# Output weights of an attention block asked for earlier, between the transposes of the last head

## The chip, the cores and the metric

The kernel runs on one core of one Trainium2 chip. The metric is the device time of one execution in microseconds (us). The core has a matrix engine (TensorE, PE), a vector engine (VectorE, DVE), an activation engine (ScalarE, ACT), a general engine (GpSimd, POOL) and a sync engine (SyncE, SP) whose queue issues DMA transfers. Each engine runs its own instructions in order; semaphores tie them together.

## The reference

A transformer block on x of 1 x 2048 x 512 in float32: modulation vectors from a conditioning vector, layer norm, causal attention with 16 heads of 128, its output projection and residual, a second layer norm, and a mixture of 64 experts (top 4) with shared experts. The change touches only the end of the attention:

```
q, k, v = h @ Q_w[hd] + Q_b[hd], h @ K_w[hd] + K_b[hd], h @ V_w[hd] + V_b[hd]     # per head hd, 16 heads
p    = softmax(where(causal, q @ k.T / sqrt(128), -1e5))
attn = p @ v                                                                       # 2048 x 128 per head
x    = x + ga * (sum over hd of attn[hd] @ O_w[hd] + O_b)                          # O_w[hd]: 128 x 512
```

## The kernel before, in words

Every product is made from high and low parts with three matmuls (`matmul3`, L1696 to L1698). A head is worked in four stages j = 0 to 3, one for each block of 512 query rows. In a stage, TensorE first computes the scores of block j (`strip`), then the attended values of block j-1 (`sum_values`, written to `pv`), then q, k and v of the next block (`gen`). VectorE takes the scores out of PSUM with their maxima (L1257, L1263, L1267), ScalarE takes exponentials in place (`exps`, L935) and writes the high half of the probabilities (`p_hi`, L944), VectorE the low half (`p_lo`, L1281). Both halves are transposed by DMA into `pT` (L500, `turn_first_rows` for the first two of the four row tiles, `turn_last_rows` for the others), and v by another (L528, `turn_values`). ScalarE takes attended values out of `pv` into the single buffer `at_f` (L950, `attended`), which it may overwrite only once the store of the block before has landed (`at_stored`; L533, `store_at`). In ScalarE's order q and k of the next block (L922, L924) come behind that, and VectorE's `kT_lo` (L1210) behind those; the scores of the next stage need it.

All of these transfers stand in the queue of SyncE, in the order in which the code writes them, and so do the 16 output weight tiles `O_w[hd]`, 256 KB each (`load_wo`, L560). They go through three raw buffers (`wq_raw`, `wk_raw`, `wv_raw`, tile hd in buffer hd % 3), so the request for tile hd first waits until GpSimd has split tile hd-3 (`wo_split`). GpSimd's split is a cast (L834) and a subtraction (L836) into `wo`; tiles 0 to 7 may be written once v of block 0 of the last head is computed, tiles 8 to 15 once v of its block 3 is. While a request waits, nothing behind it in SyncE's queue is issued.

The last head is head 15, written (15, j) below for its stage j. After the scores of (15, 3) and the attended values of (15, 2), TensorE begins the output projection: 16 row tiles i, each the sum over 16 heads, 48 matmuls of `wo` and `a_hi`/`a_lo`. Row tile i = 0 waits for `wo_split` of hd + 1 before each head's three matmuls, the last of them for tile 15. Then come i = 1, the attended values of (15, 3), i = 2 and so on. The attended heads are read back from `at_dram` in units u of four heads (`load_a`, L584 into `a_early` for u < 6, L588 into the two buffers `a_f` after that), and split by ScalarE (`take_a`, L1021, which waits for `a_used` of four units before) and VectorE (`split_a`, L1432). ScalarE takes out the attended values of (15, 3) behind unit 11, SyncE stores them and then loads x again for the residual (`load_xo`, L591), on which GpSimd adds a bias row by row (L843), on which VectorE's sum (L1446) waits.

Of the kernel before, what the change touches and what calls it, by code (L numbers as in the profile page):

```python
# [41 lines left out]
def adaln_block(nc, x, Q_w, Q_b, K_w, K_b, V_w, V_b, O_w, O_b, Wr, router_bias, Wg, Wu, Wd, Sg, Su, Sd,  # L42
                c_in, wmod, out):
    _, S, D = x.shape
    H, _, DH = Q_w.shape
    E, _, HE = Wg.shape
    NS, _, HS = Sg.shape
    TOPK = 4
# [18 lines left out]
    with ExitStack() as ctx:  # L67
# [122 lines left out]
        def wo_raw(hd):  # L190
            return raw[hd % WOS][:].rearrange("p c d -> p (c d)")
# [186 lines left out]
        def groups_before(j):  # L378
            return j * (j + 1) // 2
# [9 lines left out]
        def slot_free(n, h):  # L389

            before = n + GROUPS - PTS if n >= PTS else n + (GROUPS - 1 - n) // PTS * PTS
            return h * GROUPS + (before + 1)
# [66 lines left out]
        def _(sp):  # L459
            def wait_alone(semaphore, value):  # L460

                sp.wait_ge(semaphore, value)
                sp.sem_inc(sp_waited, 1)
# [32 lines left out]
            def turn_pair(h, j, r, g, part):  # L496

                rows = (p_hi16, p_lo16)[part][:, g, 2 * r:2 * r + 2, :].rearrange("p t c -> p (t c)")
                out = pT[:, slot_of(j, g), part, 2 * r:2 * r + 2].rearrange("p t k q -> p (t k) q")
                sp.dma_start_transpose(out, rows).then_inc(p_turned[slot_of(j, g)], 16)  # L500

            def turn_first_rows(h, j):

                wait_alone(p_hi, h * NT + (TB * j + 2))
                for g in range(j + 1):
                    wait_alone(pv_group, slot_free(groups_before(j) + g, h))
                    turn_pair(h, j, 0, g, 0)
                if j == 1:
                    turn_values(h, 1, h)
                wait_alone(p_lo, h * NT + (TB * j + 2))  # L510
                for g in range(min(j + 1, QB - 1)):
                    turn_pair(h, j, 0, g, 1)

            def turn_last_rows(h, j):
                wait_alone(p_hi, h * NT + (TB * j + 4))
                for g in range(j + 1):
                    if g == QB - 1:
                        turn_pair(h, j, 0, g, 1)
                    turn_pair(h, j, 1, g, 0)
                    if g == 0:  # L520
                        wait_alone(p_lo, h * NT + (TB * j + 4))
                    turn_pair(h, j, 1, g, 1)

            def turn_values(h, j, ready):
                wait_alone(gen_out, nth("v", j, ready) + GENS)
                if j == 0 and not (isinstance(h, int) and h == 0):
                    wait_alone(pv_group, h * GROUPS + (groups_before(QB - 1) + 1))
                sp.dma_start_transpose(v16[:, j].rearrange("p n t d -> p (n t) d"), vT16[:].rearrange("p n c -> p (n c)")  # L528
                                       ).then_inc(v_turned, 16)

            def store_at(h, j):
                wait_alone(at_ready, h * QB + (j + 2))
                sp.dma_start(at_dram[bass.ds(h, 1), :, 512 * j:512 * j + 512].rearrange("o p s -> (o p) s"), at_f[:]  # L533
                             ).then_inc(at_stored, 16)
# [20 lines left out]
            def load_wo(hd):  # L555
                if hd < WOS:
                    sp.wait_ge(w_split, 3 * H)
                else:
                    sp.wait_ge(wo_split, hd - WOS + 1)
                sp.dma_start(wo_raw(hd), O_w[hd]).then_inc(wo_landed[hd % WOS], 16)  # L560

            turn_first_rows(H - 1, 1)
            turn_last_rows(H - 1, 1)
            for hd in range(6):
                load_wo(hd)
            store_at(H - 1, 0)
            turn_values(H - 1, 2, H - 1)
            for hd in range(6, 9):
                load_wo(hd)
            turn_first_rows(H - 1, 2)  # L570
            for hd in range(9, 12):
                load_wo(hd)
            turn_last_rows(H - 1, 2)
            store_at(H - 1, 1)
            turn_values(H - 1, 3, H - 1)
            load_wo(12)

            at_parts = at_dram.rearrange("(n h) p s -> n p h s", h=HH)

            def load_a(u):  # L580
                i, part = u // TU, u % TU
                src = at_parts[part][:, :, P * i:P * i + P]
                if u < EARLY:
                    sp.dma_start(a_early[:, u], src).then_inc(a_early_landed[u], 16)  # L584
                    return
                if u >= EARLY + AFS:
                    sp.wait_ge(a_split, u - AFS + 1)
                sp.dma_start(a_f[:, u % AFS], src).then_inc(a_landed[u % AFS], 16)  # L588
# [27 lines left out]
            sp.wait_ge(at_stored, 16 * (QB * h + 2))  # L616
            for u in range(EARLY):
                load_a(u)
            for hd in range(13, H):
                load_wo(hd)  # L620
            turn_first_rows(h, j)
            sp.wait_ge(strip_done, NSTRIP * H)
            for u in range(EARLY, EARLY + AFS):
                load_a(u)
            turn_last_rows(h, j)
            store_at(h, QB - 2)
            sp.wait_ge(wo_split, H - 1)
            sp.dma_start(gob[:], O_b.partition_broadcast(P)).then_inc(ob_landed, 16)
            for u in range(EARLY + AFS, UNITS):
# [1436 lines left out]
```

## Time and profile before

| what | value |
|---|---|
| median of 3 runs | 2032.54 us (2032.47 to 2037.23) |
| profiled execution, its own time | 2040.55 us |
| its span | 2038.9 us |
| PE busy | 1942.8 us (95%) |
| DVE, ACT, POOL busy | 1422.5, 1121.6, 568.8 us |
| mean granted TensorE clock | 0.985 |

TensorE is busy for 95% of the span. In the profile's 40 slices of 51 us its busy digit is 9 nearly everywhere; the lowest after the beginning is a 6 in the slice from 1274 to 1325 us, where the clock's digit is 7 too, and the slice behind it has an 8. These two hold the last stages of head 15 and the start of the output projection. Before 1226 us the heads repeat one pattern; the stages of head 15 begin with its scores at 1227 us (stage 0), 1246 (stage 1), 1260 (stage 2) and 1287 (stage 3). The output projection begins at 1317 us.

In a timeline row the columns are start, duration, engine, line and tiles, and in brackets the idle time before it and what ended that. A row with SPq is the issue of a DMA on SyncE's queue.

### The profile page before, as it was taken

To read this page: it belongs to the slowest core of one execution; us is meant where nothing else is said; L and a number is where in the kernel's file an instruction comes from. 1 tells how busy PE (TensorE), PEld (TensorE's weight loads), DVE (VectorE), ACT (ScalarE), POOL (GpSimd) and SP (SyncE) were. 2 spreads that over 40 slices of the span, in tenths; PEclk is the share of its full clock that TensorE was granted. 3 is DMA by queue.
4 is the path that set the end of the run, shared out by engine and by line. 5 is a ranking of instruction groups with operands and counts; after the bars stand their busy time and mean duration, and the time that the engine had idled before them with its cause. 6 is when DMAs were issued, how large, how long until landed. Compare 5 with 4: busy or idle time off the path is not lost.

```text
span 2038.9 us, 33861 instructions
## 1 busy us (share of the span) xinstructions
PE 1942.8 (95%) x9821; PEld 1147.9 (56%) x9821; DVE 1422.5 (70%) x3593; ACT 1121.6 (55%) x1638; POOL 568.8 (28%) x585
## 2 busy tenths in 40 slices
PE   5899999999999999999999999689999999999998
PEld 2444444444444444444444444368877778777786
DVE  5787797797797797797797797546545843333477
ACT  3576776776676676676676676413333144344311
POOL 5430330330330330330330311632000132222265
PEclk8999999999999999999999999799999999999999
DMA  6278777777777777777777777874431098999676
GB/s 237 64 173 176 172 173 176 172 173 176 172 172 176 173 172 176 178 168 176 175 171 176 172 156 160 206 207 142 124 109 32 1 294 276 314 293 312 223 209 185
DMA packets 932246, 366.68 MB, mean 180 GB/s; under 512 B 754800, under 2 KB 885920, under 8 KB 932128
## 3 DMA queue, kind: packets, MB, share of 16 engines
q1 hardware_dynamic: 921888, 331.93, 64.9%
q0 software_dynamic: 10240, 33.56, 5.3%
q14 instruction: 90, 0.74, 0.1%
q8 instruction: 28, 0.46, 0.1%
HBM read 138.86 MB, written 41.94 MB: 89 GB/s over the span
## 4 chain that ended last, share of the span: by engine, by line
PE 66%; DVE 8%; DMA 6%; SPq 6%; issue 6%; POOL 4%; ACT 3%; DVEq 0%; ACTq 0%; POOLq 0%
PE gen L1696 9%; PE gen L1697 9%; PE gen L1698 9%; PE strip L1696 6%; PE strip L1698 6%; PE strip L1697 6%; PE pv L1697 5%; PE pv L1696 5%; PE pv L1698 5%; SPq L500 5%; PE strip L2005 4%; DMA wd_sb<-in_L_ffn_Wd 3%; DVE p_lo L1281 2%; PE strip L2012 2%; POOL gath L887 2%
## 5 line engine op out<-in xcount | busy, mean ns | idle before, releaser
L935 ACT ACTIVATE exps<-exps,nbias,cols_now 128x128 f32<-128x128 f32 (+15 forms) x256 | 329.8, 1288 | 176.2 <-DVE cmin L1267 174.2
L1281 DVE SCALAR_TENSOR_TENSOR p_lo<-exps,rinv,p_hi 128x512 f16<-128x512 f32 (+3 forms) x256 | 404.5, 1606 | 26.2 <-ACT p_hi L944 25.2
L944 ACT ACTIVATE p_hi<-exps,rinv 128x512 f16<-128x512 f32 (+3 forms) x256 | 335.4, 1352 | 37.2 <-issue 15.7
L1257 DVE TENSOR_SCALAR_CACHE_REDUCE exps<-strip 128x512 f32<-128x512 f32 x384 | 250.9, 687 | 128.2 <-PE strip L1698 127.2
L1696 PE MATMUL strip<-kT_hi,qT_hi 128*128 128x512 f16 (+3 forms) x640 | 221.1, 350 | 30.7 <-DVE kT_lo L1210 21.6
L1696 PE MATMUL pv<-pT,v 128*128 128x512 f16 (+3 forms) x640 | 223.3, 349 | 3.5 <-DMA pT<-p_lo 3.5
L1697 PE MATMUL strip<-kT_lo,qT_hi 128*128 128x512 f16 (+3 forms) x640 | 223.6, 349 | 0.0
L1697 PE MATMUL pv<-pT,v 128*128 128x512 f16 (+3 forms) x640 | 223.3, 349 | 0.0
L1698 PE MATMUL strip<-kT_hi,qT_lo 128*128 128x512 f16 (+3 forms) x640 | 221.2, 349 | 0.0
L757 POOL TENSOR_TENSOR wq_f<-wq_f,fac 128x512 f32<-128x512 f32 x16 | 16.7, 1041 | 730.7 <-PE gen L1698 726.8
L1698 PE MATMUL pv<-pT,v 128*128 128x512 f16 (+3 forms) x640 | 219.8, 349 | 0.0
L1120 ACT ACTIVATE xbT<-gen,modT,scale_b 128x128 f32<-128x128 f32 x256 | 96.4, 457 | 89.2 <-PE gen L1997 89.2
L1696 PEld LDWEIGHTS strip<-kT_hi,qT_hi 128*128 128x128 f16 x640 | 62.7, 98 | 118.0 <-issue 36.5
L1263 DVE CUSTOM_DVE_ANT_0 exps<-strip,causal 128x128 f32<-128x128 f32 (+3 forms) x256 | 124.6, 487 | 5.2 <-PE strip L1698 2.4
L1642 DVE TENSOR_TENSOR hE<-strip,sil_e 128x128 f32<-128x128 f32 x64 | 18.7, 292 | 150.2 <-ACT sil_e L1127 84.9
L1696 PE MATMUL gen<-wo,a_hi 128*128 128x512 f32 x256 | 101.5, 396 | 10.7 <-DVE a_lo L1432 5.7
L950 ACT ACTIVATE at_f<-pv,at_bias,at_scale 128x512 f32<-128x512 f32 x64 | 49.0, 765 | 105.6 <-PE pv L1698 98.2
L1021 ACT ACTIVATE a_hi<-a_f 128x512 fp32r<-128x512 f32 x58 | 36.6, 632 | 123.3 <-DMA a_f<-at_dram 86.6
L1696 PEld LDWEIGHTS pv<-pT,v 128*128 128x128 f16 x640 | 62.8, 98 | 70.1 <-issue 5.6
L1696 PE MATMUL gen<-hT_hi,wq_hi 128*128 128x512 f16 x256 | 97.7, 382 | 3.7 <-issue 3.7
L1697 PE MATMUL gen<-wo,a_hi 128*128 128x512 f32 x256 | 100.5, 393 | 0.0
L1698 PE MATMUL gen<-wo,a_lo 128*128 128x512 f32 x256 | 100.4, 392 | 0.0
(266 smaller groups left out, 4309.5 us busy)
## 6 DMA issues: line engine op xcount, KB each, us to landing
at_dram<-at_f SPq DMA_DIRECT2D x64, 256.0 KB, 2.5
wg_sb<-in_L_ffn_Wg SPq DMA_DIRECT2D x64, 256.0 KB
wu_sb<-in_L_ffn_Wu SPq DMA_DIRECT2D x64, 256.0 KB
wd_sb<-in_L_ffn_Wd SPq DMA_DIRECT2D x64, 256.0 KB
yb_dram<-yb SPq DMA_DIRECT2D x64, 256.0 KB
a_f<-at_dram SPq DMA_DIRECT2D x58, 256.0 KB, 2.8
pT<-p_hi SPq DMA_TRANSPOSE x320, 2.7
pT<-p_lo SPq DMA_TRANSPOSE x320, 2.8
```

Of the source, the lines that this page charges most:

```text
L500: sp.dma_start_transpose(out, rows).then_inc(p_turned[slot_of(j, g)], 16)
L935: nc.scalar.activation(row, row, ACT.Exp, bias=nbias[:, t:t + 1], scale=cols_now[:, LOGIT_UP:LOGIT_UP + 1], accum_out=rsum[:, t:t + 1]).th ...
L944: nc.scalar.activation(p_hi16[:, 0:j + 1, t, :], row, ACT.Copy, scale=rinv[:, t:t + 1]).then_inc(p_hi, 1)
L950: nc.scalar.activation(at_f[:], pv[:], ACT.Identity, bias=at_bias[:, 0:1], scale=at_scale[:, 0:1]).then_inc(at_ready, 1)
L1120: ins = nc.scalar.activation(xbT[:, i % 2, P * ch:P * ch + P], e_turn[:, P * ch:P * ch + P], ACT.Identity, bias=modT[:, 3 * DC + ch:3 * DC ...
L1257: nc.vector.tensor_scalar(exps[:, t, 512 * ch:512 * ch + w], strip[u % STRIPS][:, 0:w], 1.0, None, ALU.mult, ALU.max, accum_out=cmax[:, t, ...
L1263: nc.vector.tensor_tensor_reduce(exps[:, t, 512 * ch:512 * ch + w], strip[u % STRIPS][:, 0:w], causal[:, TB * P - w:TB * P], 1.0, -3e38, A ...
L1281: nc.vector.scalar_tensor_tensor(p_lo16[:, 0:j + 1, t, :], row, rinv[:, t:t + 1], p_hi16[:, 0:j + 1, t, :], ALU.mult, ALU.subtract).then_i ...
L1696: nc.tensor.matmul(o, a_hi, b_hi, start=start, stop=False)
L1697: nc.tensor.matmul(o, a_hi, b_lo, start=False, stop=False)
L1698: return nc.tensor.matmul(o, a_lo, b_hi, start=False, stop=stop)
L2005: last = nc.tensor.matmul(e_gateup[i % 2][:, P * n:P * n + P], w[:, i % EX, c, :], xbT[:, i % 2, P * c:P * c + P], start=c == 0, stop=c == ...
```

## The change

The order of SyncE's queue changes in the last head; no instruction is added or taken away. Requests for weight tiles now stand as follows: tiles 0 to 2 ahead of the first transposes of (15, 1); 3 and 4 between its first and last ones; 5 to 7 behind the store of (15, 0) and the transposition of v; 8 and 9 between the first and last transposes of (15, 2); 10 to 12 behind the six `a_early` loads; 13 and 14 behind the two `a_f` loads, between the first and last transposes of (15, 3); and 15 behind its last ones and the store of (15, 2).

```diff
+            for hd in range(3):
+                load_wo(hd)
             turn_first_rows(H - 1, 1)
+            for hd in range(3, 5):
+                load_wo(hd)
             turn_last_rows(H - 1, 1)
-            for hd in range(6):
-                load_wo(hd)
             store_at(H - 1, 0)
             turn_values(H - 1, 2, H - 1)
-            for hd in range(6, 9):
+            for hd in range(5, 8):
                 load_wo(hd)
             turn_first_rows(H - 1, 2)
-            for hd in range(9, 12):
+            for hd in range(8, 10):
                 load_wo(hd)
             turn_last_rows(H - 1, 2)
             store_at(H - 1, 1)
             turn_values(H - 1, 3, H - 1)
-            load_wo(12)
...
             for u in range(EARLY):
                 load_a(u)
-            for hd in range(13, H):
+            for hd in range(10, 13):
                 load_wo(hd)
             turn_first_rows(h, j)
             sp.wait_ge(strip_done, NSTRIP * H)
             for u in range(EARLY, EARLY + AFS):
                 load_a(u)
+            for hd in range(13, 15):
+                load_wo(hd)
             turn_last_rows(h, j)
             store_at(h, QB - 2)
+            load_wo(H - 1)
             sp.wait_ge(wo_split, H - 1)
```

SyncE's queue before, from the end of the transposes of (15, 1) to the transposition of v for (15, 2):

```order
L500 DMA_TRANSPOSE pT<-p_lo_118 128x8x128
L560 DMA wq_raw<-in_L_attn_O_w 128x512
L560 DMA wk_raw<-in_L_attn_O_w 128x512
L560 DMA wv_raw<-in_L_attn_O_w 128x512
L560 DMA wq_raw<-in_L_attn_O_w 128x512
L560 DMA wk_raw<-in_L_attn_O_w 128x512
L560 DMA wv_raw<-in_L_attn_O_w 128x512
L533 DMA at_dram<-at_f 128x512
L528 DMA_TRANSPOSE v_113<-vT_114 128x8x128
```

Six requests stood ahead of the store of (15, 0), the last three of them with a wait for GpSimd. The same place now, from the end of the first transposes of (15, 1):

```order
L500 DMA_TRANSPOSE pT<-p_lo_118 128x8x128 x2
L560 DMA wq_raw<-in_L_attn_O_w 128x512
L560 DMA wk_raw<-in_L_attn_O_w 128x512
L500 DMA_TRANSPOSE pT<-p_hi_117 128x8x128
L500 DMA_TRANSPOSE pT<-p_lo_118 128x8x128
L500 DMA_TRANSPOSE pT<-p_hi_117 128x8x128
L500 DMA_TRANSPOSE pT<-p_lo_118 128x8x128
L533 DMA at_dram<-at_f 128x512
L528 DMA_TRANSPOSE v_113<-vT_114 128x8x128
L560 DMA wv_raw<-in_L_attn_O_w 128x512
L560 DMA wq_raw<-in_L_attn_O_w 128x512
L560 DMA wk_raw<-in_L_attn_O_w 128x512
```

The two requests shown first are tiles 3 and 4; the store now follows the transposes directly. The queue before, around the first transposes of (15, 3), where tiles 13 to 15 were requested:

```order
L584 DMA a_early<-at_dram 128x4x128 x6
L560 DMA wk_raw<-in_L_attn_O_w 128x512
L560 DMA wv_raw<-in_L_attn_O_w 128x512
L560 DMA wq_raw<-in_L_attn_O_w 128x512
L500 DMA_TRANSPOSE pT<-p_hi_117 128x8x128 x4
L500 DMA_TRANSPOSE pT<-p_lo_118 128x8x128 x3
L588 DMA a_f<-at_dram 128x4x128 x2
L500 DMA_TRANSPOSE pT<-p_hi_117 128x8x128
```

The last of the three `wq_raw`/`wk_raw`/`wv_raw` rows is tile 15. The end of the last transposes of (15, 3) now:

```order
L500 DMA_TRANSPOSE pT<-p_lo_118 128x8x128 x2
L500 DMA_TRANSPOSE pT<-p_hi_117 128x8x128
L500 DMA_TRANSPOSE pT<-p_lo_118 128x8x128
L533 DMA at_dram<-at_f 128x512
L560 DMA wq_raw<-in_L_attn_O_w 128x512
L632 DMA gob<-in_L_attn_O_b 128x512
L589 DMA a_f<-at_dram 128x4x128 x5
```

The `wq_raw` row is tile 15; it has moved behind all 16 transposes of (15, 3), two `a_f` loads and the store of (15, 2).

## Rows read from the trace of the kernel before

**Rows 1.** Windows by stage: stretch, length, busy (instructions) of PE, PEld, DVE, ACT, POOL, clock, DMA, GB/s.
```profile
1287.09:1299.04 11.95, 11.85 (x48) 5.01 (x48) 9.12 (x38) 3.84 (x4) 5.43 (x7) 0.82 0.97 225
1302.56:1312.26 9.70, 9.70 (x36) 4.04 (x36) 2.23 (x1) 4.26 (x3) 2.39 (x2) 0.70 1.04 224
1317.45:1330.62 13.17, 13.17 (x49) 10.71 (x49) 11.77 (x8) 6.92 (x8) 10.41 (x6) 0.82 1.02 209
1330.62:1341.50 10.88, 10.88 (x49) 8.82 (x48) 0.69 (x1) 0.63 (x1) 0.00 (x0) 1.00 1.02 188
1341.50:1350.88 9.38, 9.38 (x49) 4.55 (x49) 1.39 (x2) 1.26 (x2) 1.27 (x1) 1.00 0.60 144
```

**Rows 2.** Timeline of PE: start, duration, engine, line, tiles, idle time before.
```profile
1287.09 0.61 PE L1696 MATMUL strip<-kT_hi,qT_hi 128*128 128x512 f16 x1 [8.00 <-DVE kT_lo L1210]
...
1302.56 0.58 PE L1696 MATMUL pv<-pT,v 128*128 128x512 f16 x1 [3.53 <-DMA pT<-p_lo]
...
1317.45 0.77 PE L1696 MATMUL gen<-wo,a_hi 128*128 128x512 f32 x1 [5.02 <-issue]
...
1341.50 0.39 PE L1696 MATMUL pv<-pT,v 128*128 128x512 f16 x1
...
1367.32 0.50 PE L1696 MATMUL gen<-wo,a_hi 128*128 128x512 f32 x1 [2.54 <-DVE a_lo L1432]
```

**Rows 3.** Timeline of ACT in the last head.
```profile
1267.62 3.04 ACT L944 ACTIVATE p_hi<-exps,rinv 128x1536 f16<-128x1536 f32 x2 [1.42 <-issue]
...
1284.23 0.78 ACT L950 ACTIVATE at_f<-pv,at_bias,at_scale 128x512 f32<-128x512 f32 x1 [7.44 <-issue]
...
1308.00 3.89 ACT L944 ACTIVATE p_hi<-exps,rinv 128x2048 f16<-128x2048 f32 x2 [11.23 <-DMA pT<-p_lo]
...
1315.85 1.13 ACT L1021 ACTIVATE a_hi<-a_early 128x512 fp32r<-128x512 f32 x2
```

**Rows 4.** Timeline of SyncE's DMA issues in the last head.
```profile
1265.65 0.58 SPq L560 DMA_DIRECT2D wq_raw<-in_L_attn_O_w x1
...
1280.41 0.33 SPq L560 DMA_DIRECT2D wv_raw<-in_L_attn_O_w x1
1280.85 0.36 SPq L533 DMA_DIRECT2D at_dram<-at_f x1
...
1286.62 4.01 SPq L500 DMA_TRANSPOSE pT<-p_hi x3
...
1314.30 0.43 SPq L560 DMA_DIRECT2D wq_raw<-in_L_attn_O_w x1
...
1340.82 0.50 SPq L533 DMA_DIRECT2D at_dram<-at_f x1
```

**Rows 5.** Waits of SyncE, 1200 to 1400 us: total, times, longest.
```profile
SPq L560 <- POOL wo L836: 15.3, 6, 5.0
```

**Rows 6.** Tile `wo`: GpSimd's casts and subtractions, ns least/median/most, first and last start.
```profile
L834 POOL CAST wo<-wv_raw x5: 607/611/2677, 1275.4 to 1319.7; 128x512 fp32r<-128x512 f32 x5
L836 POOL TENSOR_TENSOR wo<-wv_raw,wo x5: 1264/1266/2653, 1277.7 to 1322.5; 128x512 fp32r<-128x512 f32 x5
```

**Rows 7.** Line L560 (weight requests), 1264 to 1270 us, then 1312 to 1330: time to landing.
```profile
DMA to landing us min/median/max: 3.0/3.3/3.7
...
DMA to landing us min/median/max: 4.5/4.5/4.7
```

**Rows 8.** Timeline of POOL: the split of tile 0 and the end of tile 15's.
```profile
1269.46 2.72 POOL L836 TENSOR_TENSOR wo<-wq_raw,wo 128x512 fp32r<-128x512 f32 x1
...
1326.81 1.62 POOL L836 TENSOR_TENSOR wo<-wq_raw,wo 128x512 fp32r<-128x512 f32 x1
```

**Rows 9.** Timeline of DVE: low halves in stages (15, 1) and (15, 2).
```profile
1256.11 2.58 DVE L1281 SCALAR_TENSOR_TENSOR p_lo<-exps,rinv,p_hi 128x1024 f16<-128x1024 f32 x2
...
1269.23 1.82 DVE L1281 SCALAR_TENSOR_TENSOR p_lo<-exps,rinv,p_hi 128x1536 f16<-128x1536 f32 x1
```

**Rows 10.** Chain that ended last, 1341 to 1363 us: start, duration, what.
```profile
1352.85 0.77 ACT at_f L950
...
1354.10 8.27 DMA acc<-in_L_attn_x
```

## The prediction

> **What bounds the kernel now.** I read the table of 40 slices first, since PE is busy for 95% of the span and only a hole in its row can be won: the hole is at 1274 to 1350 us, the last stages of head 15. Then the timeline of PE there, for what ended each idle time [rows 2]: 8.00 us ahead of the scores of (15, 3), 3.53 ahead of the attended values of (15, 2), 5.02 ahead of the output projection, 16.6 us together. The windows by stage [rows 1] show that each gap is followed by a stretch at a mean granted clock of 0.82, 0.70 and 0.82, between the levels 2.4 and 1.2 GHz; that loses 0.18 x 11.95 + 0.30 x 9.70 + 0.18 x 13.17 = 7.4 us. So 24 us is the most that this stretch could give.
>
> The waits of SyncE [rows 5] and its issues [rows 4] name the cause of the first gap: weight requests wait 15.3 us for GpSimd's splits, the sixth request (tile 5) is out at 1280.41, and the store of (15, 0) behind it at 1280.85. `at_f` may be overwritten only after that store, so ScalarE stands 7.44 us up to 1284.23 [rows 3], and q and k of block 3 stand behind it. From 1286.62 on SyncE has no wait of weight on requests left: it is the transposes that fill its queue up to the store of (15, 2), 1286.62 to 1340.82 + 0.50 = 1341.32 [rows 4], 54.7 us. ScalarE's 11.23 us up to 1308.00 are a wait for them [rows 3].
>
> **Moving tiles 0 to 7.** The store of (15, 0) no longer stands behind waiting requests. The three requests ahead of the first transposes of (15, 1) cost nothing, since SyncE was waiting there for `p_hi`. Tiles 3 and 4 need the splits of 0 and 1, which land some 3 us after 1248 and take 0.61 + 1.27 us each [rows 6, 7]: done by about 1257, before SyncE comes to them at 1259. They cost 2 x 0.5 us of issue ahead of the last transposes. ScalarE's first `p_hi` of (15, 2) idled 1.42 us [rows 3] and I read this as a wait for those transposes, so it starts 1 us later and its second row tile is ready at 1267.62 + 3.04 + 1.0 = 1271.7. The first transposes of (15, 2) go at 1271.8 instead of 1286.62. The store now goes at about 1267; ScalarE is then free for `at_f` when its own `p_hi` are done, 7 us earlier less the 1 us. What is late next is SyncE itself.
>
> **The queue from there on.** Between the first transposes of (15, 2) and the store of (15, 2) the queue holds the same before and after: 29 transposes, 8 loads of attended values, 2 stores, 7 weight requests (before 9 to 15, now 8 to 14). With the durations of before the store ends at 1271.8 + 54.7 = 1326.5. Without any congestion it is 29 x 1.34 (4.01 for three, rows 4) + 17 x 0.58 (the longest plain issue in rows 4) = 48.7 us, so 1320.5. I take 1324.5, between them: the loads that crowd the rings, six units of `a_early` and three weights, still stand directly ahead of transposes.
>
> **Moving tile 15.** This is the edit that decides. Before, tile 15 was requested at 1314.30 [rows 4], ahead of the transposes of (15, 3), and its split ended at 1326.81 + 1.62 = 1328.43 [rows 8], 2.2 us before row tile 0 of the projection ended at 1330.62 [rows 1]. It now stands behind all those transposes and the store. Requested at 1324.5; landing 3.0 to 4.7 us [rows 7], I take 3.6, nearer to the row measured behind transposes; split 0.61 + 0.08 + 1.27 = 1.96 [rows 6]: ready at 1330.1. TensorE needs it much sooner. The last transposes of (15, 2) are issued 8.1 + 1.0 + 8.1 = 17.2 us after 1271.8 and land some 2 us after that, 1291.1, so `p_hi` of (15, 3) comes 16.9 us earlier than 1308.00, `a_hi` at 1315.85 - 16.9 = 1299 [rows 3], the projection at 1300.6 instead of 1317.45 [rows 2]. Its row tile 0 gets to head 15 at about 1314 and stands 16 us. In place of three gaps there is one of the same size.
>
> **The sum.** From 1330.1 TensorE has 3 matmuls of head 15 and 48 of row tile 1, at 10.88 / 48 = 0.227 us [rows 1] 11.6 us, and restarts at the low level: the stretches after the three gaps lost 2.15, 2.9 and 2.4 us, I take 2.3. The attended values of (15, 3) start at 1330.1 + 13.9 = 1344.0; before 1341.50 [rows 2]. That is 2.5 us late. They take 9.38 us [rows 1].
>
> Something comes back behind them. Before, they ended at 1350.88 but ScalarE took them out at 1352.85 [rows 10], since in its order they stand behind unit 11, whose load SyncE could not ask for before 1341. These loads now start at about 1325 and are there; `at_f` comes at 1344.0 + 9.38 + 0.25 = 1353.6, 0.8 us later than before. This instruction releases the store, the load of x (8.27 us, rows 10) and GpSimd's bias, and VectorE's sums behind that are what TensorE idles for at 1367.32 (2.54 us, rows 2) and twice more shortly after. So TensorE's own 2.5 us are taken out of those idles and 0.8 us stays. Nothing later is touched. In the profiled execution's terms 2040.55 + 0.8 = 2041.4; the median of the runs is 8.0 us below that execution, and I put the same 0.8 on it: 2033.3 us.
>
> **Bounds.** Low: store at 1320.5, landing 3.0, split 1.96, 11.6, no clock loss: 1337.1, 4.4 before 1341.50, with the 1.7 of the loads (1352.85 less 1350.88 + 0.25) 6.1 early. High: 1326.5, landing 4.7, both GpSimd operations at their contended ends 0.61 + 2.65 = 3.3 [rows 6], 11.6, clock 2.9: 1349.0, 7.5 late less 1.7 is 5.8 late. So 2026.4 to 2038.3.
>
> The landing time has a second price. Beside the 3.0 to 4.7 us measured, the Trainium skill (DMA: Bandwidth & Descriptors, the anatomy of one DMA) fits about 2.0 us plus the bytes over 436 GB/s for the other path of issue, which for 256 KB is 2.6 us, by estimate. By that, tile 15 would be 1.0 us earlier and the forecast 2032.3; the rows show no landing under 3.0, so the trace does not agree.
>
> **Rivals.**
>
> *GpSimd's splits collide with VectorE in stage (15, 1): slower.* Splits of tiles 0 to 2 now fall at 1251 to 1260 us, where VectorE has no idle time and makes `p_lo` [rows 9]. A subtraction of GpSimd that met `p_lo` of 1269.23 took 2.72 us against 1.27 [rows 6, 8, 9], ending about 1.2 us after it: one holds the other off. If three subtractions each hold VectorE for their 1.27 us, the chain to `p_hi` of (15, 2) is 3.8 us later, and one starved split in front of a waiting request (2.7 us) is added to SyncE's queue. All of it goes onto tile 15: 0.8 + 3.8 + 2.7 = 7.3 us slower, 2039.8. It decides as soon as the first transposes of (15, 2) go later than about 1277. Against it: the wait for landing there hides the first 1 us or more, and TensorE's slack behind. The Trainium skill has this as a rule (SBUF — State Buffer, the shared pair of ports: a VectorE instruction with two SBUF inputs and a GpSimd one that reads SBUF exclude each other for the whole instruction); so far the trace agrees, with 2.72 against 1.27.
>
> *Tile 15 is not what TensorE waits for: faster.* Then row tiles 0 and 1 run from 1300.6 to about 1323, the attended values of (15, 3) follow as their transposes land and end near 1333, 17 us before 1350.88: 2032.5 - 17 = 2015.5. For it: all gaps of rows 2 are closed. Against it: even the uncongested queue gives the request no earlier than 1320.5, and row tile 0 can't end without that tile. To be over 6.1 us faster needs it about 1 us sooner than my lowest case, with no clock loss.
>
> *The store was not what ScalarE stood for at 1284.23* (the row names no releaser). Then the gap ahead of (15, 3) stays and the projection starts at about 1311 instead of 1300.6; but it stands for tile 15 all the same, and the end is as forecast, 2033.3 or 1 us more by what `p_hi` of (15, 3) would be late.
>
> **Chances.** Forecast 0.68, collision 0.15, faster 0.09, store not the cause 0.08. A change of 0.3%, 6.1 us, is about what can be told from none. Beyond it to the slow side lie most of the collision's case and 0.03 of the forecast's tail: 0.16. Beyond it to the fast side 0.08 and 0.02: 0.10. Within it 0.74. The range: the forecast's own bounds, drawn in a little below and reaching on the slow side to the collision, 2027 to 2039.5.
>
> **What would show it.** Right: the store of (15, 0) at about 1267; no idle time over 3 us ahead of the scores of (15, 3) and none ahead of the attended values of (15, 2); the projection starting near 1301; one idle time of TensorE of 12 to 18 us inside its row tile 0, ended by GpSimd's split of tile 15 out of `wq_raw` at 1327 to 1334, and a granted clock under 0.9 after it; SyncE with less than 3 us of waits for GpSimd in all. Wrong: that idle time under 8 us, or the split of tile 15 before 1322; or `p_lo` of (15, 1) stretched beyond 1.27 us a piece and the scores of (15, 3) not before 1286. And wrong in the last step, if the load of x comes later than `at_f` explains, or TensorE keeps its idle times at 1367 us beside the later start.

## The result, and the profile after

The changed kernel takes 2041.98 us (median of 20 executions, 2036.35 to 2045.09); the kernel before, run beside it on the same chip, takes 2038.72 us (20 executions, 2032.47 to 2041.54). The ratio is 1.0016 with a 95% interval of 1.0009 to 1.0023: some 3.3 us slower, within the 0.3% that was named as no change. Forecast were 0.8 us more, on a base of 2032.5 us. The base was wrong by itself: it was the median of three executions, and 20 have their median 6 us higher. The profiled executions are 2040.55 us before and 2043.57 us after (spans 2038.9 and 2042.0), which is 3.0 us more; the traces can be compared directly, except that the one of after runs 0.47 us late already at the store of (14, 3), 1247.83 against 1247.36.

The timeline of PE after, for the places of [rows 2]; in the brackets the idle time before the instruction and what ended it:

```profile
1262.60 0.39 PE L1700 MATMUL strip<-kT_hi,qT_hi 128*128 128x512 f16 x1 [2.43 <-DVE kT_lo L1214]
...
1284.07 0.39 PE L1700 MATMUL strip<-kT_hi,qT_hi 128*128 128x512 f16 x1 [2.49 <-DVE kT_lo L1214]
...
1303.42 0.47 PE L1700 MATMUL gen<-wo,a_hi 128*128 128x512 f32 x1 [1.01 <-issue]
...
1312.04 0.50 PE L1700 MATMUL gen<-wo,a_hi 128*128 128x512 f32 x1 [0.89 <-POOL wo L840]
...
1314.81 0.47 PE L1700 MATMUL gen<-wo,a_hi 128*128 128x512 f32 x1 [1.81 <-POOL wo L840]
...
1320.01 0.80 PE L1700 MATMUL gen<-wo,a_hi 128*128 128x512 f32 x1 [4.11 <-POOL wo L840]
...
1334.10 0.80 PE L1700 MATMUL gen<-wo,a_hi 128*128 128x512 f32 x1 [10.54 <-POOL wo L840]
...
1348.22 0.39 PE L1700 MATMUL pv<-pT,v 128*128 128x512 f16 x1
...
1375.43 0.50 PE L1700 MATMUL gen<-wo,a_hi 128*128 128x512 f32 x1 [1.22 <-DVE a_lo L1436]
```

The gaps of 8.00 and 3.53 us are gone: 2.43 us stand ahead of the scores of (15, 2), 2.49 us are left ahead of the scores of (15, 3) and none ahead of the attended values of (15, 2). The projection starts at 1303.42 instead of 1317.45, 14 us earlier, and then stands 17.6 us in its row tile 0, each time for a split of `wo`; the last and longest, 10.54 us, is for tile 15. The attended values of (15, 3) begin at 1348.22, against 1341.50 before. The windows by stage (length, busy and count of PE, PEld, DVE, ACT, POOL, then clock, DMA share, GB/s) say the same, to be read beside [rows 1]: stage (15, 3)'s scores and what follows, the projection up to tile 15, and the rest of it.

```profile
1284.07:1303.42 19.35, 18.24 (x85) 8.44 (x85) 17.00 (x53) 13.94 (x13) 3.85 (x5) 0.91 1.02 248
1303.42:1334.10 30.68, 13.07 (x46) 8.73 (x46) 12.28 (x8) 6.07 (x8) 16.60 (x13) 0.70 0.94 204
1334.10:1347.10 13.00, 13.00 (x47) 10.53 (x48) 2.76 (x4) 2.53 (x4) 1.24 (x1) 0.80 0.22 63
```

TensorE is busy for 13.07 of 30.68 us in the second, at a mean granted clock of 0.70, and works the third at 0.80.

SyncE's issues after, for [rows 4]: start, duration, line, what is issued and how often.

```profile
1268.24 0.51 SPq L533 DMA_DIRECT2D at_dram<-at_f  x1
...
1273.51 3.94 SPq L500 DMA_TRANSPOSE pT<-p_hi  x3
...
1300.29 7.21 SPq L500 DMA_TRANSPOSE pT<-p_hi  x4
...
1315.37 3.15 SPq L500 DMA_TRANSPOSE pT<-p_lo  x1
...
1328.32 0.51 SPq L533 DMA_DIRECT2D at_dram<-at_f  x1
1328.87 0.43 SPq L560 DMA_DIRECT2D wq_raw<-in_L_attn_O_w  x1
```

The store of (15, 0) goes 12.6 us earlier than in [rows 4], and the first transposes of (15, 2) 13.1 us earlier. But from them to the end of the store of (15, 2) it is 1328.83 - 1273.51 = 55.3 us, no less than the 54.7 before. The request of tile 15, at 1314.30 before, is out at 1328.87. Of what waited 15.3 us in [rows 5] nothing is left: the waits of SyncE after show no wait of a weight request for GpSimd. What GpSimd does (timeline of POOL, for [rows 8]) is this:

```profile
1254.26 2.13 POOL L840 TENSOR_TENSOR wo<-wk_raw,wo 128x512 fp32r<-128x512 f32 x1
...
1258.02 2.13 POOL L840 TENSOR_TENSOR wo<-wv_raw,wo 128x512 fp32r<-128x512 f32 x1
...
1332.09 0.61 POOL L838 CAST wo<-wq_raw 128x512 fp32r<-128x512 f32 x1 [10.24 <-DMA wq_raw<-in_L_attn_O_w]
1332.78 1.26 POOL L840 TENSOR_TENSOR wo<-wq_raw,wo 128x512 fp32r<-128x512 f32 x1
...
1365.95 24.94 POOL L847 TENSOR_TENSOR acc<-acc,gob 128x512 f32<-128x512 f32 x16 [30.61 <-DMA acc<-in_L_attn_x]
```

and ScalarE (timeline of ACT, for [rows 3] and [rows 10]):

```profile
1270.30 3.04 ACT L948 ACTIVATE p_hi<-exps,rinv 128x1536 f16<-128x1536 f32 x2 [1.62 <-issue]
...
1279.38 0.76 ACT L954 ACTIVATE at_f<-pv,at_bias,at_scale 128x512 f32<-128x512 f32 x1
...
1293.23 3.88 ACT L948 ACTIVATE p_hi<-exps,rinv 128x2048 f16<-128x2048 f32 x2
...
1357.83 0.78 ACT L954 ACTIVATE at_f<-pv,at_bias,at_scale 128x512 f32<-128x512 f32 x1 [8.73 <-PE pv L1702]
```

The 7.44 and 11.23 us of idle time of [rows 3] are gone, and `p_hi` of (15, 3) comes 14.8 us earlier. All of it is spent by 1357.83, where `at_f` comes 5.0 us later than at 1352.85 in [rows 10].

### The profile page after: what moved, and what is told of

The parts are those of the page before. It is cut to its first block, busy times and chain, and to the rows that moved or that the text cites. A ratio compares the mean times of both kernels' runs of the same rounds, so it can differ in the third digit from the quotient of the medians.

```text
span 2042.0 us, 33859 instructions
## 1 busy us (share of the span) xinstructions
PE 1941.5 (95%) x9819; PEld 1148.7 (56%) x9821; DVE 1427.3 (70%) x3593; ACT 1120.8 (55%) x1638; POOL 568.6 (28%) x585
## 4 chain that ended last, share of the span: by engine, by line
PE 71%; DVE 8%; SPq 5%; DMA 5%; issue 5%; ACT 3%; POOL 3%; ACTq 0%; DVEq 0%; POOLq 0%
PE gen L1700 9%; PE gen L1702 9%; PE gen L1701 9%; PE strip L1700 7%; PE strip L1702 6%; PE strip L1701 6%; PE pv L1702 5%; PE pv L1700 5%; PE pv L1701 5%; PE strip L2009 4%; SPq L500 4%; DMA wd_sb<-in_L_ffn_Wd 2%; DVE p_lo L1285 2%; PE strip L2016 2%; POOL acc L847 1%
## 5 line engine op out<-in xcount | busy, mean ns | idle before, releaser
L1700 PE MATMUL gen<-wo,a_hi 128*128 128x512 f32 x256 | 102.4, 400 | 21.4 <-POOL wo L840 17.6
L1436 DVE TENSOR_TENSOR a_lo<-a_f,a_hi 128x512 fp32r<-128x512 f32 x58 | 45.9, 794 | 79.5 <-ACT a_hi L1025 79.3
```

What stands on the lines that cost most here:

```text
L1700: nc.tensor.matmul(o, a_hi, b_hi, start=start, stop=False)
```

## The experiments

All ratios are to the kernel before, run beside each on the same chip. Two theories stood against each other at the start: *tile 15* (its request behind the last transposes and the store eats what the other moves free) and *collision* (GpSimd's splits, now in stage (15, 1), hold VectorE off and make everything later).

### Tile 15 requested with tiles 13 and 14

```
             for u in range(EARLY, EARLY + AFS):
                 load_a(u)
-            for hd in range(13, 15):
+            for hd in range(13, 16):
                 load_wo(hd)
             turn_last_rows(h, j)
             store_at(h, QB - 2)
-            load_wo(H - 1)
```

> The changed kernel with tile 15 requested together with tiles 13 and 14, between the first and last transposes of (15, 3), instead of behind them. Theory (the place of tile 15 in SyncE's queue eats the gain): its split ends near 1324 us instead of 1334, the idle time of 10.5 us in row tile 0 shrinks to under 3 us, ScalarE takes out the attended values of (15, 3) near 1347 instead of 1357.8, and the time is 10 us below the changed kernel and 6 to 7 us below the kernel before (ratio 0.9965, between 0.995 and 0.998). Rival (the transposes of (15, 3) set the end in any case): TensorE waits as long again ahead of the attended values of (15, 3), ratio 1.0016 as the changed kernel.

Measured: 2031.33 us against 2037.86; ratio 0.9965 (0.9955 to 0.9976). Against the 1.0016 of the changed kernel this one line is worth 0.51%, some 10.4 us. PE's timeline:

```profile
1318.89 0.79 PE L1699 MATMUL gen<-wo,a_hi 128*128 128x512 f32 x1 [5.54 <-POOL wo L839]
...
1322.71 0.79 PE L1699 MATMUL gen<-wo,a_hi 128*128 128x512 f32 x1 [0.26 <-POOL wo L839]
...
1381.11 1.94 PE L1774 MATMUL strip<-ident,n 128*128 128x128 f32 x16 [0.35 <-DVE n L1183]
```

In place of 10.54 us TensorE waits 0.26 us for the split that is last, tile 15's, which ends at 1322.65. The last row, the first turns for the second normalization, is a mark behind the stretch: 1381.11 here, 1390.81 in the kernel before, 1394.31 in the changed one. The collision is still in this kernel (its four `p_lo` of (15, 1) take 7.25 us), and it is faster nevertheless. The wait of 5.54 us shown first is for tile 13, 4.11 us in the changed kernel. So tile 15 decides the sign.

### The late tile alone, in the kernel before

```
-            for hd in range(13, H):
+            for hd in range(13, H - 1):
                 load_wo(hd)
...
             store_at(h, QB - 2)
+            load_wo(H - 1)
```

> The kernel before with one edit: tile 15 is requested behind the last transposes of (15, 3) and the store of (15, 2), as in the changed kernel; tiles 0 to 14 as before. Theory (the two parts of the change are gates on one path, so the late tile costs more where nothing else was gained): tile 15 is requested at 1341 and split near 1346 where it was at 1328.4, TensorE stands 15 to 17 us for it, and some 14 us of that stay, ratio 1.007 (1.006 to 1.009). Rival (the parts add up): the loss is what e1 gains over the changed kernel, 0.51%, ratio 1.005.

Measured: 2051.38 us against 2037.16; ratio 1.0069 (1.0056 to 1.0082), some 14 us slower. The request is out at 1338.14 and the split done at 1343.42, each some 3 us sooner than expected, and TensorE stands 14.38 us for it. The PE timeline keeps the first gap of before, and has the one for tile 15 beside it:

```profile
1284.96 0.61 PE L1697 MATMUL strip<-kT_hi,qT_hi 128*128 128x512 f16 x1 [6.45 <-DVE kT_lo L1211]
...
1343.47 0.79 PE L1697 MATMUL gen<-wo,a_hi 128*128 128x512 f32 x1 [14.38 <-POOL wo L837]
...
1403.02 1.94 PE L1772 MATMUL strip<-ident,n 128*128 128x128 f32 x16 [0.37 <-DVE n L1181]
```

Whether the two parts add up is not settled. The first experiment gives 0.35%, the late tile alone costs 0.69%, and the two together cost 0.16% where 0.34% would be the sum; by the intervals that sum is 0.17 to 0.51%, which overlaps the 0.09 to 0.23% measured. Nor are the parts quite the same: against the kernel before tile 15's split ends 15.0 us later here (1343.42 for 1328.43), and in the changed kernel 11.4 us later than in the first experiment (1334.04 for 1322.65).

### The store alone put ahead of the requests

```
             turn_last_rows(H - 1, 1)
+            store_at(H - 1, 0)
             for hd in range(6):
                 load_wo(hd)
-            store_at(H - 1, 0)
```

> The kernel before with one edit: the store of (15, 0) goes ahead of the requests for tiles 0 to 5 instead of behind them; all else as before. Theory (the length of SyncE's queue is the bound, the store only decides which gap is seen): the 8.0 us of TensorE ahead of the scores of (15, 3) fall to under 3 us, the first transposes of (15, 2) still go near 1286, and the idle time ahead of the attended values of (15, 2) grows from 3.5 to 9 us or so; ratio to before 1.000 +- 0.001. Rival (the store behind the waiting requests was the whole loss): the projection starts 6 to 8 us earlier and the time falls by 6 to 8 us, ratio 0.9965.

Measured: 2039.3 us; ratio 1.0008 (0.9999 to 1.0017), no difference. PE:

```profile
1281.64 0.39 PE L1696 MATMUL strip<-kT_hi,qT_hi 128*128 128x512 f16 x1 [2.21 <-DVE kT_lo L1210]
...
1302.43 0.59 PE L1696 MATMUL pv<-pT,v 128*128 128x512 f16 x1 [10.28 <-DMA pT<-p_lo]
...
1317.24 0.77 PE L1696 MATMUL gen<-wo,a_hi 128*128 128x512 f32 x1 [6.54 <-issue]
```

The gap ahead of (15, 3) falls from 8.00 to 2.21 us, so the store was what ScalarE stood for; the next gap grows from 3.53 to 10.28 us. In SyncE's timeline the first transposes of (15, 2) go at 1287.64, no earlier than the 1286.62 of [rows 4], since the requests still wait there for splits. A gap that closes ahead of an unmoved one is handed on to it.

```profile
1287.64 3.95 SPq L500 DMA_TRANSPOSE pT<-p_hi  x3
...
1339.86 0.50 SPq L533 DMA_DIRECT2D at_dram<-at_f  x1
```

From there on this queue holds the same as that of the kernel before, in the same order, and its stretch up to the store of (15, 2) is 1340.36 - 1287.64 = 52.7 us, against 54.7 before. So one trace's reading of that stretch is good to about 2 us.

### The bytes of the requests taken away

In the changed kernel, tiles 3 to 15 ask for the first 32 of 512 columns alone, 16 KB in place of 256 KB; the other 480 columns of each are not loaded, and the projection is computed with those of the tiles before.

```
-                sp.dma_start(wo_raw(hd), O_w[hd])...
+                cols = slice(0, D if hd < WOS else 32)
+                sp.dma_start(wo_raw(hd)[:, cols], O_w[hd][:, cols])...
```

> The changed kernel, but the requests for tiles 3 to 15 fetch only the first 32 of 512 columns (the other columns of the output weights are those of the tiles before); the number and order of all instructions stays. Theory (the bytes of the requests crowd the rings and stretch the transposes): the stretch from the first transposes of (15, 2) to the store of (15, 2) falls from 55.3 to about 51 us, tile 15 is split near 1329 instead of 1334, ratio 0.999. Rival (the transposes and the loads of attended values crowd them by themselves): the stretch stays within 1 us of 55.3, only the landing of tile 15 gets shorter by 0.5 us or so, ratio 1.001 to 1.0015.

Measured: 2037.18 us; ratio 0.9999 (0.999 to 1.0008). SyncE's timeline, for the changed kernel's:

```profile
1273.27 3.94 SPq L500 DMA_TRANSPOSE pT<-p_hi  x3
...
1298.85 5.37 SPq L500 DMA_TRANSPOSE pT<-p_hi  x4
...
1311.95 1.24 SPq L500 DMA_TRANSPOSE pT<-p_lo  x1
...
1323.00 0.51 SPq L533 DMA_DIRECT2D at_dram<-at_f  x1
```

The stretch is 1323.51 - 1273.27 = 50.2 us in place of 55.3. Of the 5.1 us, 3.75 lie in two places behind requests (four transposes take 5.37 us in place of 7.21, one 1.24 in place of 3.15), and 0.7 is a wait of SyncE for `vT` that the changed kernel has and this one has not. Beside the 52.7 us of the experiment before, which has the large requests, it is 2.5 us; so the requests' bytes cost 2.5 to 5 us of the stretch, by estimate, and one trace on each side does not tell more closely. Tile 15's split still comes last, with 9.33 us of idle time on TensorE ahead of 1328.47. Its place in the queue, not its size, makes most of that wait.

### Splits moved out of VectorE's way

The first experiment's kernel, with tiles 0 to 2 requested ahead of stage (15, 0), so that their splits fall at 1241 to 1247 us:

```
-            for hh, j, prev, nxt in stages(H - 2, False):
+            for hh, j, prev, nxt in stages(H - 2, False)[:-1]:
                 stage(hh, j, prev, nxt)
...
             for hd in range(3):
                 load_wo(hd)
+            stage(*stages(H - 2, False)[-1])
```

> The kernel of e1 (the changed one with tile 15 beside tiles 13 and 14) with tiles 0 to 2 requested one stage earlier, ahead of stage (15, 0) in SyncE's queue, so that their splits fall where VectorE has 8.6 us of idle time. Theory (GpSimd's splits hold VectorE off in stage (15, 1)): TensorE's idle time ahead of the scores of (15, 2), 2.49 us in e1 and 0.42 before, goes back to under 0.6, the first transposes of (15, 2) come 1 to 2 us earlier after stage (15, 1), ratio to before 0.9955 to 0.996 against 0.9965 of e1. Rival (those 2 us come from the requests that stand ahead of transposes, not from the splits): the idle time stays over 2 us and the ratio is 0.9965 or more.

Measured: 2027.97 us against 2037.16; ratio 0.9951 (0.9938 to 0.9965), beside 0.9965 (0.9955 to 0.9976) with the collision. The intervals overlap, so its price in time is not settled. That it is there shows in VectorE's `p_lo` of (15, 1), first with the collision (the changed kernel), then without:

```profile
1253.68 1.58 DVE L1285 SCALAR_TENSOR_TENSOR p_lo<-exps,rinv,p_hi 128x1024 f16<-128x1024 f32 x1
...
1255.44 2.03 DVE L1285 SCALAR_TENSOR_TENSOR p_lo<-exps,rinv,p_hi 128x1024 f16<-128x1024 f32 x1
...
1257.65 3.58 DVE L1285 SCALAR_TENSOR_TENSOR p_lo<-exps,rinv,p_hi 128x1024 f16<-128x1024 f32 x2
```

```profile
1252.89 1.28 DVE L1285 SCALAR_TENSOR_TENSOR p_lo<-exps,rinv,p_hi 128x1024 f16<-128x1024 f32 x1
...
1254.34 1.26 DVE L1285 SCALAR_TENSOR_TENSOR p_lo<-exps,rinv,p_hi 128x1024 f16<-128x1024 f32 x1
...
1255.78 2.59 DVE L1285 SCALAR_TENSOR_TENSOR p_lo<-exps,rinv,p_hi 128x1024 f16<-128x1024 f32 x2
```

7.19 us in place of 5.13. TensorE's wait ahead of (15, 2) falls from the 2.49 us of the first experiment to 0.42, but the one ahead of (15, 3) grows to 3.30, and SyncE's first transposes of (15, 2) follow the store of (14, 3) by 1272.19 - 1247.09 = 25.1 us instead of 25.7. ScalarE, which no longer waits for VectorE, waits 3.10 us instead of 1.62 ahead of its `p_hi` of (15, 2). So of the 2.1 us about 0.6 reach the queue in these traces, less than the 1 to 2 us expected. That is a low reading: one of the transposes ahead took 2.60 us there (at 1261.54) and 1.38 in the first experiment.

### The requests in GpSimd's queue

The kernel before, with all 16 requests issued by GpSimd and none by SyncE:

```
             split_weights(H - 1)
+            pool.wait_ge(w_split, 3 * H)
+            for hd in range(WOS):
+                load_wo(hd)
             for hd in range(H):
...
                                         ).then_inc(wo_split, 1)
+                if hd + WOS < H:
+                    pool.wait_ge(wo_split, hd + 1)
+                    load_wo(hd + WOS)
```

> The kernel before with all 16 weight requests issued by GpSimd itself (tiles 0 to 2 after its last weight split, tile hd+3 after the split of tile hd), none in SyncE's queue. Theory (SyncE's queue is the bound of the last head): the first transposes of (15, 2) go near 1271, the stretch from there to the store of (15, 2) shortens by 4 us or more from 54.7 us, no wait of TensorE for a split, attended values of (15, 3) taken out near 1336, ratio 0.992 (0.990 to 0.995). Rival (GpSimd's requests and its early splits collide with VectorE, which has no idle time in the stages 0 and 1): VectorE's low halves stretch by over 5 us in all and the ratio is 0.998 or more.

Measured: 2025.11 us; ratio 0.9941 (0.9928 to 0.9954), some 12 us under the kernel before, the lowest ratio of all, though its interval overlaps that of the experiment above. The profiled execution is one of the faster ones (2021.97 us). GpSimd's and SyncE's rows, then PE's:

```profile
1209.73 0.80 POOL L816 DMA_DIRECT2D wq_raw<-in_L_attn_O_w  x1 [0.32 <-POOL wv_lo L746]
1210.53 0.56 POOL L816 DMA_DIRECT2D wk_raw<-in_L_attn_O_w  x1
```

```profile
1272.86 3.94 SPq L500 DMA_TRANSPOSE pT<-p_hi  x3
...
1299.01 7.35 SPq L500 DMA_TRANSPOSE pT<-p_hi  x4
...
1324.42 0.51 SPq L533 DMA_DIRECT2D at_dram<-at_f  x1
```

```profile
1252.07 0.47 PE L1689 MATMUL pv<-pT,v 128*128 128x512 f16 x1 [2.63 <-DMA pT<-p_lo]
...
1303.17 0.54 PE L1689 MATMUL gen<-wo,a_hi 128*128 128x512 f32 x1 [3.94 <-issue]
...
1373.53 1.94 PE L1764 MATMUL strip<-ident,n 128*128 128x128 f32 x16 [0.39 <-DVE n L1173]
```

Each tile is requested when the split before has freed its buffer; tile 15's split is done at 1308.5, 20 us before the 1328.43 of before, and TensorE waits for no split. The mark is at 1373.53, 17 us before 1390.81. A request costs GpSimd 0.56 us (0.80 the first). SyncE's stretch is 52.1 us, 2.6 or 0.6 shorter than the 54.7 and 52.7 us measured for the queue of before, where at least 4 were expected and the issues of its 7 requests alone took 3.5. The transposes and loads in it take longer instead: the six `a_early` loads are issued in 6.81 us (4.24 before) and the four transposes behind them in 7.35 (6.72 before), while the bytes of the last tiles, requested up to 1296.23, are under way.

The rival is seen too: the four `p_lo` of (15, 0) take 5.91 us in place of 2.73, beside splits, and TensorE waits 0.51 and 2.63 us for transposes in the stages (15, 0) and (15, 1), where it had no wait before. What the edit gains elsewhere is much more than that. It does two things at once, and they were not tried apart: no request stands in SyncE's queue any more, and the tiles are requested earlier, the first at 1209.73.

## Why the prediction was right and wrong

**Two steps of the sum failed.** The time is 2041.98 us where 2033.3 was forecast, 8.7 more. Of these, 6.2 us are the base: I put the kernel before at 2032.5 us, and it takes 2038.72 (more under *the level*). The other 2.5 us are the difference, 3.3 us where I had 0.8; that step is the time at which tile 15 is ready (below). Without the first the range would not have missed: as a difference it reaches from 5.5 us faster to 7.0 slower.

**The mechanism held in the main.** One long wait in row tile 0 of the projection for tile 15's split took the place of the gaps, the store released ScalarE, SyncE lost its waits for GpSimd, and the chance of 0.74 was on a difference within 0.3%. That tile 15 decides is shown by its move alone: 10.4 us on top of the other moves, 14 us without them. The rival in which it is not the gate falls with that; the one in which the store is not the cause falls with the 8.00 us that became 2.21.

**The difference was off by 2.5 us, and the step is the time at which tile 15 is ready**: forecast 1330.1, measured 1332.78 + 1.26 = 1334.0, 3.9 late. Its terms:
- Start of the queue, 1273.51 instead of 1271.8: 1.7 late. 0.47 is the profiled execution's own lateness. About 0.6 is the collision, by the experiment that moves the splits. The last 0.6 is not told apart.
- The stretch, 55.3 instead of 52.7 us: 2.6 late, the larger part. I had taken the queue to run freer than before, and nothing shows that it does. The requests' bytes are 2.5 to 5 us of it, by the experiment with small requests; moving requests within the stretch does not take them away, and taking them out of this queue gave 52.1 us. But 52.7 is also what one trace of the unmoved queue gave, so up to 2 of these 2.6 us may be what traces differ by; no run settles that.
- The landing, 3.1 instead of 3.6 us: 0.5 early. The estimate of 2.6 us from the Trainium skill (DMA: Bandwidth & Descriptors, the anatomy of one DMA) is under this row. I had written that the trace does not agree with it, from the two windows of [rows 7]; three requests of the same kernel, issued at 1272 to 1281 us (DMA share 0.35 there), landed in 2.5 to 3.0 us, so there it does agree.
- The split, 1.96 us: right. In the slow bound, though, "contended ends" took the cast at 0.61 us, its shortest; its longest is 2.68 [rows 6]. That bound should have been 2.1 us higher.

**The end.** The attended values of (15, 3) start 4.2 us later than forecast, and `at_f` is 1357.83 - 1352.85 = 5.0 late instead of 0.8. From there the forecast left no room for change. But the load of x landed in 6.72 us instead of the 8.27 of [rows 10], GpSimd began its bias at 1365.95 instead of 1362.51, and the mark behind is at 1394.31, 3.5 late: 1.5 us of the 5.0 came back. Why that load was faster was not tried. That the error in the difference stayed at 2.5 us, with tile 15 3.9 us late, is therefore in part luck.

**The collision is real, but as a rival it was priced far too high.** GpSimd's two subtractions take 2.13 us in place of 1.27 and VectorE's `p_lo` 7.19 in place of 5.12 (1.27 + 1.27 + 2.58, the last in [rows 9]), and TensorE's 2.43 us ahead of the scores of (15, 2), 0.42 before, are what is seen of it. The Trainium skill has such a pair of instructions exclude each other (SBUF — State Buffer, the shared pair of ports); the trace agrees in that both sides take longer. Forecast were 3.8 us for VectorE and 2.7 for a starved split, 6.5 us in the queue. Measured is 2.1 us on VectorE, some 0.6 of which reach the queue in the traces compared, and no request waits. The first transposes went at 1273.5, well before the 1277 from which it was to decide.

**The projection came to its tiles otherwise than said.** I forecast one wait of 16 us at about 1314. There are 10.54 us for tile 15 and 7.1 us before and beside it for the splits of the tiles ahead, 17.6 together. I had followed the request of tile 15 alone. The timeline of POOL of the changed kernel shows what was late of the others:

```profile
1307.64 1.07 POOL L838 CAST wo<-wv_raw 128x512 fp32r<-128x512 f32 x1
1308.79 3.19 POOL L840 TENSOR_TENSOR wo<-wv_raw,wo 128x512 fp32r<-128x512 f32 x1
1311.93 1.07 POOL L838 CAST wo<-wq_raw 128x512 fp32r<-128x512 f32 x1
...
1318.00 0.61 POOL L838 CAST wo<-wk_raw 128x512 fp32r<-128x512 f32 x1 [3.34 <-DMA wk_raw<-in_L_attn_O_w]
```

The waits of 0.89 and 1.81 us end as two splits do that took 4.3 and 2.7 us instead of 1.9, the one of 4.11 us as that of a tile which landed only at 1318.00. That these splits were slow because VectorE was then busy with stage (15, 3) is by analogy with stage (15, 1); it was not tried. The kernel before has such splits in that stage as well: those of tiles 14 and 15 took 4.4 us each, beside two `p_lo` of 3.03 and 3.38 us where the first two of that stage take 2.35 and 2.33.

**The level.** The range, 2027 to 2039.5 us, misses 2041.98 since its base stood on three executions with a median of 2032.5. The profiled execution, 8 us above them, was within 2 us of the 2038.7 that 20 executions give. An execution so far from a median of three says that the median is not known to better than that distance.

## What to carry to other kernels

Where requests are moved within one queue, write down when each of their consumers wants its data and check the last one as well: a late request behind a full queue costs as much as all the earlier ones gain (here 10 us and 7). A request that has to wait for another engine's work is better issued by that engine, where it holds up no unrelated transfer; here that was worth 12 us, together with the earlier requests. And count the bytes apart from the issues: here the transposes behind the requests were issued more slowly, whichever engine had asked for the bytes. Before reading 2 us out of one trace, look what a second trace of the same queue gives.

## What was not expected of the hardware

- Behind requests of 256 KB the issue of one DMA transpose takes SyncE up to 3.15 us in the stretch from the first transposes of (15, 2) to the store of (15, 2) (4.38 us in the kernel of the first experiment), and there at most 1.34 us, the mean of the four in 5.37, with requests of 16 KB. With the requests issued by GpSimd four take 7.35 us, so it is not the queue of the issuer alone. Bytes of weight tiles are not the only cause: in the run with small requests one takes 1.92 us at 1236.52, before any tile is requested, and one 2.18 us at 1264.51. What holds up these two was not tried.
- A cast of GpSimd, which reads one tile, is stretched too where it falls beside `p_lo`: 1.61 us in place of 0.61 in stage (15, 1) of the changed kernel, and 2.15 us (at 1275.50) in (15, 2). [rows 6] had it already, with a longest cast of 2.68 us; the prediction counted subtractions alone.
